# Two feed-forward units moved into the delta-rule recurrence, and the gate projection of the second batch moved between the parts of P @ u

## The reference

```python
xn = layernorm(x)
x + attention(xn) + feed_forward(xn)

# attention: 16 heads, key size 16, value size 32
q, k, v = silu(causal_conv4(xn @ W_qkv)); q, k = l2norm(q) * SCALE, l2norm(k)
beta = 2 * sigmoid(xn @ W_b + biases);  g = -exp(A_log) * softplus(xn @ W_a + dt_bias)
for t: S = S * exp(g_t); S += outer(k_t, (v_t - k_t @ S) * beta_t); o_t = q_t @ S
o = o * rsqrt(mean(o*o) + eps) * silu(xn @ W_g);  return o @ W_o

# feed forward: weights are 4-bit codes with one scale for 128 inputs; 1408 hidden features
h = silu(xn @ W_gate) * (xn @ W_up);  y = h @ W_down;  return y / sqrt(mean(y*y) + 1e-6)
```

## Time and profile before

| | |
|---|---|
| median of three runs | 3354.63 us |
| the profiled execution's own time | 3358.53 us |
| its span, first to last instruction | 3356.7 us |
| mean granted TensorE clock | 0.988 |
| busy: PE, DVE, ACT, POOL | 94%, 73%, 50%, 55% |
| chain that ended last, by engine | PE 64%, DVE 14%, issue 8%, POOL 6%, ACT 4% |

### The profile page before, as it was taken

One profiled execution on the slowest core, in us unless ns is written; L12 is line 12 of the kernel. 1 busy time (PEld: TensorE's weight loads), 2 busy tenths in 40 slices (PEclk: granted clock), 3 DMA queues, 4 the chain that ended last, 5 costly groups with the idle time before them and its releaser, 6 DMA issues.

```text
span 3356.7 us, 118358 instructions
## 1 busy us (share of the span) xinstructions
PE 3167.9 (94%) x45632; PEld 2247.1 (67%) x45632; DVE 2434.3 (73%) x5407; ACT 1666.1 (50%) x3306; POOL 1838.7 (55%) x2737
## 2 busy tenths in 40 slices
PE   4899999999999999999999999999999999999995
PEld 3666666766666766666666667666667666667663
DVE  7777777777777777777777777777777777777772
ACT  3444554545554445555445545455545455544452
POOL 3565455665455664456654456654556654456542
PEclk8999999999999999999999999999999999999996
DMA  3111111111111111111111111111111111111111
GB/s 111 39 46 27 34 44 35 45 38 28 40 40 39 46 33 30 43 33 45 46 27 37 43 33 45 45 28 34 43 36 46 37 28 42 37 42 46 33 25 30
DMA packets 318316, 132.07 MB, mean 39 GB/s; under 512 B 277088, under 2 KB 278880, under 8 KB 317792
## 3 DMA queue, kind: packets, MB, share of 16 engines
q1 hardware_dynamic: 313824, 119.26, 14.3%
q10 hardware_dynamic: 4096, 6.42, 0.5%
HBM read 75.30 MB, written 50.33 MB: 37 GB/s over the span
## 4 chain that ended last, share of the span: by engine, by line
PE 64%; DVE 14%; issue 8%; POOL 6%; ACT 4%; DMA 1%; ACTq 1%; DVEq 1%; SPq 0%; POOLq 0%
PE PS L1145 15%; PE PS L1210 7%; PE PS L1132 7%; PE PS L1133 6%; PE PS L1351 6%; PE PS L1100 5%; DVE arena L874 4%; PE PS L1275 3%; POOL arena L497 3%; POOL work L493 2%; DVE qkv L858 2%; DVE inner L976 2%; PE PS L1228 2%; PE PS L1196 2%; PE PS L1246 2%
## 5 line engine op out<-in xcount | busy, mean ns | idle before, releaser
L874 DVE SCALAR_TENSOR_TENSOR arena<-PS,sc,arena 128x256 f32<-128x256 f32 x2112 | 1004.5, 482 | 291.9 <-ACT arena L594 191.8
L1132 PE MATMUL PS<-xh,wgu 128*128 128x256 f32 x2816 | 872.0, 341 | 36.1 <-DVE arena L874 35.5
L594 ACT ACTIVATE arena<-PS,sc 128x256 f32<-128x256 f32 x704 | 330.8, 475 | 757.7 <-PE PS L1133 701.8
L1133 PE MATMUL PS<-xl,wgu 128*128 128x256 f32 x2816 | 699.3, 282 | 0.0
L1145 PE MATMUL PS<-wdn,inner 128*128 128x512 f32 x1408 | 650.7, 592 | 0.0
L1132 PEld LDWEIGHTS PS<-xh,wgu 128*128 128x128 f32 x2816 | 531.3, 189 | 156.2 <-issue 83.5
L1133 PEld LDWEIGHTS PS<-xl,wgu 128*128 128x128 f32 x2816 | 530.5, 188 | 83.2 <-issue 83.2
L497 POOL TENSOR_TENSOR arena<-arena,work 128x31 f32<-128x31 f32 (+15 forms) x992 | 543.3, 548 | 77.8
L493 POOL TENSOR_TENSOR work<-arena 128x31 f32<-128x31 f32 (+15 forms) x992 | 509.8, 514 | 138.9 <-DMA arena<-scr_a 63.7
L1100 PE MATMUL PS<-xnT,wqkv 128*128 128x256 f32 x2048 | 493.3, 389 | 25.6 <-ACT inner L574 24.8
L1100 PEld LDWEIGHTS PS<-xnT,wqkv 128*128 128x128 f32 x2048 | 379.5, 192 | 105.5 <-ACT inner L574 37.8
(11 more groups left out here) (141 smaller groups left out, 4546.8 us busy)
## 6 DMA issues: line engine op xcount, KB each, us to landing
xt<-in_x SPq DMA_DIRECT2D x64, 256.0 KB, 2.8
scr_a<-arena SPq DMA_DIRECT2D x64, 256.0 KB, 2.4
arena<-scr_a SPq DMA_DIRECT2D x256, 64.0 KB, 3.3
obuf<-in_x SPq DMA_DIRECT2D x64, 256.0 KB, 2.8
scr_t<-arena SPq DMA_DIRECT2D x32, 512.0 KB, 2.7
arena<-scr_t SPq DMA_DIRECT2D x256, 64.0 KB, 2.3
out<-obuf SPq DMA_DIRECT2D x64, 256.0 KB, 2.0
wqkv<-in_wqkv ACTq DMA_DIRECT2D x1, 2048.0 KB, 12.7
```

The source lines that it names most:

```text
L594: eng.activation(fa[:, u % 4, :], PS[:, bank(u, 0), 0:NB * P], ACT.Copy, scale=sc[:, u % 2, KB * m:KB * m + 1]).then_inc(fa_scaled.sem, 1)
L874: eng.scalar_tensor_tensor(out=fa[:, u % 4, :], in0=PS[:, bank(u, k // 2), k % 2 * NB * P:][:, 0:NB * P], scalar=sc[:, u % 2, KB * m + k:K ...
L1132: eng.matmul(o, w, xh[:, k, :], start=True, stop=False)
L1133: ins = eng.matmul(o, w, xl[:, k, :], start=False, stop=True)
```

## The change

`bank` is changed so that units 0 to 3 and 5 use banks 5 and 6 and units 4 and 6 banks 4 and 7. Both batches' gate sums and the transposes `turn_kb` and `turn_kqn(1)` use bank 4, one after the other, with the waits that this needs. Units 0 and 1 are put into the last two chunks of the recurrence on PE, and unit 2 before `p_times_u(1)`. `gate(1, ...)` stands between the parts of `p_times_u`. Units 4 and 5 stand ahead of `gram(1)`, unit 6 behind it. ACT's Silu table is loaded earlier, and its queue is put in a matching order. On DVE the statistics of the next layer norm go behind `conv(2)`, the normalisation behind `hidden(6)`, units 0 and 1 around `state(3)`, and units 3 and 4 with `hidden(0)` around the key products; the sums `so` come after `hidden(1)`. `turn_o`, `to_wo` and `result` come one or two units later, `down(1)` to `down(8)` one pair of units earlier. The orders of POOL and SP are as before.

```diff
         def bank(u, fill):
-            return (6 if u in (1, 3) else 2 if u % 2 else 4) + fill
+            if u < 7:
+                return ((4, 7) if u in (4, 6) else (5, 6))[fill]
+            return (2 if u % 2 else 4) + fill
...
 ACT
             decay(1)
+            eng.preload_act_table_set(SILU)
+            masked_keys(0)
             u_rows(2)
-            masked_keys(0)
+            gate_copy(0)
+            unit(0)
             u_rows(3)
             other_keys()
-            gate_copy(0)
-            gate_copy(1)
+            unit(1)
             masked_keys(1)
             queries()
-            unit(0)
-            unit(1)
+            unit(2)
+            if n:
+                gate(0)
             if t:  # copies of the output, after pu_out
...
-            unit(2)
+            unit(3)
+            gate_copy(1)
+            if n:  # Silu of v, moved up
...
             if t:  # Square of the output
...
-            unit(3)
-            eng.preload_act_table_set(SILU)
             if n:
-                gate(0)
-                ... Silu of v
                 unit(4)
-                gate(1)
                 unit(5)
-                ... Silu of the gate
-                gate(2)
+                gate(1)
+                unit(6)
...
+            gate(2)
+            ... Silu of the gate, behind the copies of v
...
 DVE
             conv(2)
+            if n and more:
+                layer_norm_stats(eng, n.next())
...
             state(2)
-            if n and more:
-                layer_norm_stats(eng, n.next())
+            unit(0)
             state(3)
-            if n and more:
-                layer_norm_apply(eng, n.next())
+            unit(1)
             conv(6)
...
-            unit(0)
-            unit(1)
             unit(2)
+            unit(3)
             gram_products(0)
+            hidden(0)
+            unit(4)
+            gram_products(1)
+            hidden(1)
             if t:  # the sums so
...
-            gram_products(1)
-            unit(3)
-            hidden(0)
-            hidden(1)
+            unit(5)
+            hidden(2)
...
 PE, half_unit
                     if fill == 0:
-                        eng.wait_ge(*gate_copied.at(n, NB))
+                        eng.wait_ge(*decay_done.at(n, NB))
...
+                    else:
+                        eng.wait_ge(*knq_copied.at(n, 2))
-                elif u == 1: ...
-                elif u == 5:
+                elif u <= 3:
+                    eng.wait_ge(*(fa_done if fill else fa_second).at(n, u))
+                elif u == 4:
+                    eng.wait_ge(*(q_copied.at(n, 1) if fill else gate_copied.at(n, NB)))
+                elif u == 7:
                     if fill == 0:
                         eng.wait_ge(*p_done.at(n, NB))
...
 PE, the order
             gate(0, 2)
+            gate(0, 3)
             k_times_u(2)
             q_times_s(2)
-            gate(0, 3)
-            gate(1, 0)
+            unit(0)
             y_times_s(3)
             turn_kb()
+            unit(1)
+            k_times_u(3)
+            q_times_s(3)
+            turn_kqn(1)
+            p_times_u(0)
+            turn_q()
+            unit(2)
+            p_times_u(1)
+            gate(1, 0)
             gate(1, 1)
-            k_times_u(3)
+            p_times_u(2)
             gate(1, 2)
-            q_times_s(3)
+            p_times_u(3)
             gate(1, 3)
-            p_times_u(0)
-            turn_kqn(1)
-            turn_q()
-            p_times_u(1)
-            unit(0)
-            p_times_u(2)
-            unit(1)
-            p_times_u(3)
-            unit(2)
+            unit(3)
             gram(0)
-            unit(3)
+            unit(4)
+            unit(5)
             gram(1)
-            unit(4)
...
+            unit(6)
             ... transposes of v
-            unit(5)
-            unit(6)
             unit(7)
             down(0)
+            unit(8)
+            down(1)
```

More of the change, by code:

```diff
@@ L636, in gate_copy @@
                 eng.wait_ge(*gate_out.at(n, b + 1))
-                eng.activation(gsn[:, b, :], PS[:, 4 + b, :], ACT.Copy).then_inc(gate_copied.sem, 1)
+                eng.activation(gsn[:, b, :], PS[:, 4, :], ACT.Copy).then_inc(gate_copied.sem, 1)
             def masked_keys(b):
@@ L752, in act_step @@
                     eng.activation(by_pair(sq[:, b, :]), paired(1, b), ACT.Copy).then_inc(o_copied.sem, 1)
-            unit(2)
+            unit(3)
+            gate_copy(1)
+            if n:
+                eng.wait_ge(*taps_done.at(n, NQKV))
+                eng.activation(qkv[:, 4:NQKV, :], qkv[:, 4:NQKV, :], ACT.Silu).then_inc(silu_done.sem, 1)
             if t:
@@ L778, in act_step @@
                                ACT.Copy).then_inc(v_copied.sem, 1)
+            gate(2)
+            if t:
+                eng.wait_ge(*o_gated.at(t, NB))
+            eng.wait_ge(*gate_copied.at(n, NB))
+            eng.activation(gs[:, :, :], gsn[:, :, :], ACT.Silu).then_inc(gs_done.sem, 1)
             for m in range(3, FM):
-                unit(2 * m)
+                if m > 3:
+                    unit(2 * m)
                 unit(2 * m + 1)
                 gate(m)
-                if m == 4:
+                if m == 5:
                     o_columns()
@@ L1039, in dve_step @@
                 return
-            for m in range(2, FM):
+            for m in range(3, FM):
                 unit(2 * m)
@@ L1045, in dve_step @@
                 hidden(m)
-                if t and m in (6, 8):
-                    result((m - 6) // 2)
+                if more and m == 6:
+                    layer_norm_apply(eng, n.next())
+                if t and m in (7, 9):
+                    result((m - 7) // 2)
             eng.wait_ge(*res_loaded.at(n, 16 * NB))
@@ L1288, in turn_kqn @@
                 for m in range(4):
-                    ins = eng.transpose(PS[:, 6, m * P:(m + 1) * P], kqn[:, b, m * P:(m + 1) * P], ident[:, :])
+                    ins = eng.transpose(PS[:, 4 if b else 6, m * P:(m + 1) * P], kqn[:, b, m * P:(m + 1) * P], ident[:, :])
                 ins.then_inc(kqn_turned.sem, 1)
@@ L1445, in pe_step @@
                 ins.then_inc(v_turned.sem, 1)
-            unit(5)
-            unit(6)
             unit(7)
             down(0)
-            for i in range(8, NU):
+            unit(8)
+            down(1)
+            for i in range(9, NU):
                 unit(i)
                 if i % 2:
-                    down((i - 7) // 2)
-                elif i == 8:
+                    down((i - 5) // 2)
+                elif i == 10:
                     turn_o()
-                elif i <= 16:
-                    to_wo((i - 10) // 4, (i - 10) // 2 % 2)
-            down(8)
+                elif 12 <= i <= 18:
+                    to_wo((i - 12) // 4, (i - 12) // 2 % 2)
             down(9)
```

25 lines of the change are left out of this document (8 added, 17 removed).

## The result

The kernel after takes 3584.9 us (median of four runs, 3575.4 to 3592.3) against 3353.65, a ratio of 1.0684 (95% interval 1.0669 to 1.0698). The profiled execution took 3589.75 us. Forecast were 3435 (3395 to 3480): the direction was right, and the loss is 231 us where 80 were foreseen. From one `yr` to the next a tile takes 109.17 us on the mean, before 101.68; 31 x 7.5 = 232, so it is all in the steady tiles.

A forecast was written before the change was run, and what follows sets the result against it. Two rings of about 101.5 us bound it, PE's work and solve-convolution-recurrence-key products. The second grows 2.8 less 0.25 spare: 31 x 2.55 = 79, first tile about 1; 3358.5 + 80, less 3.9, gives 3435 us (3395 to 3480).

The forecast's parts named there:

- The ring: Cycle of solve, convolution, recurrence, key products and next solve, about 101.5 us, forecast to grow by 2.8 us of a tile.
- The 9.55 from `so` to the solve: On POOL, `ro` with its long power, the scaling and two memsets were to take 9.55 us before the solve.
- the last term: Per-tile sum: the solve's 2.8 us delay less 0.25 us to spare, giving 2.55 us of a tile.
- the 2.8 forecast: On POOL, the solve was to begin 2.8 us later, because `so` ends later (1.9 to 3.4 by PE's holds).
- the 0.25 to spare: When PE's feed forward ends, the solve has been over for only about 0.25 us; that much delay was free.
- PE up to unit(3): PE's order from `turn_kqn(0)` on: 1607.4 without any stall, and with 0.9 of holds unit(3) begins at 1608.3.
- the wait for banks, 0.9: Units 0 to 3 share two banks, so PE waits for DVE to end the previous unit: 0.9 us (0 to 1.5).
- The wait for DVE: PE's waits for DVE at the units, 35.5 us in all before, were to shrink.
- Rival B: Clock falls each tile as PE stands before `project(3)`: 1.1 us of a tile, 3469 us; chance 0.15.
- A: PE's ring alone counts, saving 1.2 us of a tile: 3317 us; chance 0.10.
- C: Only the key products' read back delays the solve, 0.75 us of a tile: 3378 us; chance 0.10.
- D: No change, as PE's holds and savings cancel: 3355 us; chance 0.05.

## Why the prediction was wrong

**The sizes, separated.** In the kernel with 32 matmuls in each tile no tile has a stop, and the clock falls before S + 30 not at all, for 3.4 us, or for 6.8 us. The periods fall into groups. Added to the kernel after's own, they give each piece (the first and the last tile are left out, and three that are alone of their kind):

| tiles | count | mean period |
|---|---|---|
| before, all | 31 | 101.7 |
| 32 matmuls, no stop, no fall | 9 | 104.7 (104.7 to 104.8) |
| 32 matmuls, no stop, fall of 3.4 us | 9 | 105.65 (105.55 to 105.73) |
| 32 matmuls, no stop, fall of 6.8 us | 11 | 106.8 (106.3 to 106.9) |
| 64 matmuls, stops, one fall before S + 30 | 9 | 107.3 (106.8 to 107.8) |
| 64 matmuls, stops, one fall before S + 30 and one behind | 18 | 108.9 (108.3 to 109.5) |
| after, stops, one fall before S + 30 | 2 | 108.1 (107.7 and 108.4) |
| after, stops, one fall before S + 30 and one behind | 26 | 109.2 |

Ring 3.0, first fall 0.9, stops 2.5, second fall 1.1: 7.5 us of a tile. The stops and the fall that they bring, 3.6, are 112 us of 231, the largest part. How the 3.6 is to be split is not settled: 2.5 rests on two tiles and on kernels that differ by the pad, and by the kernel with 64 matmuls it would be 1.7 for the stops and 1.6 for the fall, 3.2 together. A fall of 3.4 us takes 1.7 us of clock. The first costs 0.9, probably because a part of that slow stretch waits for others anyway, the one behind the stops 1.1 to 1.6.

**The ring was right nearly step by step.** A tile of the kernel with 32 matmuls in each tile, without stop or fall, S = 1725.15 + 0.27 = 1725.42:

```profile
1725.15 0.27 POOL L499 TENSOR_TENSOR arena<-arena,work 128x31 f32<-128x31 f32 x1
1773.10 0.68 PE L1143 MATMUL PS<-xh,wgu 128*128 128x256 f32 x1
1781.19 1.27 DVE L1039 TENSOR_REDUCE so<-qkv 128x16 f32<-128x512 f32 x2
1792.17 0.24 POOL L495 TENSOR_TENSOR work<-arena 128x31 f32<-128x31 f32 x1 [0.34 <-POOL arena L487]
1830.22 0.19 POOL L509 TENSOR_SCALAR yr<-ys 128x2 f32<-128x2 f32 x1
```

unit(3) at S + 47.7 (forecast 48.0), `so` ending at S + 57.0 (56.8), the solve starting at S + 66.75 (66.4), a period of 104.7 (101.7 + 2.55 = 104.2). The 9.55 from `so` to the solve was 9.7. The missing 0.5 is in the last term: the start moves by the 2.8 forecast (from S + 64.0 on the mean), but the 0.25 to spare does not come off, and the solve takes 38.0 us instead of 37.7. Had nothing else happened, 31 x 3.0 + 1 would have made 3449 us, within the range.

**The step that failed is "PE up to unit(3)".** It ends at "1607.4 without any stall", and the only stall then allowed for was the wait for banks, 0.9. It laid `y_times_s(3)`, `turn_kb`, unit(1), `k_times_u(3)`, `q_times_s(3)`, `turn_kqn(1)` and `p_times_u(0)` behind each other at the durations they have with gate parts between them. Four gate parts had gone from there to the places between the `p_times_u`, and with them most of the time in which the next packet of instructions can arrive. The two stops (2.5) and the clock's fall behind them (1.1) stand in this step: unit(3) begins at S + 52.1 and, in the tile without stop or fall, at S + 47.7. No term of the sum and no rival had them. The wait for DVE, which I had put in it, did shrink: 24.2 us in 66 times against 35.5.

The warning was to be had. The kernel before has 12.4 us of stops at L1275 that no partner ends, 31 times, and I passed over them as too small. They were the largest row of PE's waits that named no partner, in 20 of 31 tiles, and nearly always after the same two rows, the 55th of `p_times_u(0)` and the 37th of `p_times_u(2)`; the row of 37 at 1604.39 ends at one.

The Trainium skill (Runtime: NRT & Kernel Launch, Instruction fetch mechanics) says that an engine's instructions are refilled in blocks of 16 KiB, 256 instructions, ahead and in order, and that crossing into the next block is "mostly hidden". The size agrees with the 16.4 KB and with the pads of 256 and 128; that it is mostly hidden does not hold where PE works off 256 instructions in 3.9 us (1705.11 to 1709.02 here): it stands 1.54 us at the end of them, and 0.89 at the end of those before.

**Rival B came as well.** It was priced at 1.1 us of a tile and not taken, because PE's stop was estimated at 3.4 us, "a little less than the 3.9 in the rows". The stop was 3.9 in the tile shown and in nearly all others, and the clock was low for a time before S + 30 in each of the 31 tiles. Its price was nearly right (0.9), its chance of 0.15 too low. The comparison of 3.4 with 3.9 us was no ground for leaving the clock up: in the kernel with 64 matmuls PE stood 2.7 us, and the clock fell in nearly every tile. Nor does the length of the gap alone decide: in the kernel with 32 matmuls, two tiles have the same gap of 3.3 us, and only in the second the clock falls. PE's timeline:

```profile
1731.08 1.99 PE L1109 MATMUL PS<-xnT,wqkv 128*128 128x256 f32 x8 [3.27 <-ACT inner L576]
1835.80 6.66 PE L1109 MATMUL PS<-xnT,wqkv 128*128 128x256 f32 x16 [3.26 <-ACT inner L576]
```

Their windows, the granted clock in the third column from the end:

```profile
1732.00:1734.00 2.00, 1.61 (x8) 1.08 (x7) 1.85 (x5) 1.96 (x5) 0.00 (x0) 1.00 0.73 115
1837.00:1839.00 2.00, 2.00 (x7) 1.55 (x6) 1.78 (x6) 1.75 (x4) 0.00 (x0) 0.50 0.80 125
```

The first goes on at a clock of 1.00, the second at 0.50. The same 16 matmuls take 4.4 us in the first (two rows of 1.99 with 0.39 between) and 6.66 in the second. The rule of the Trainium skill that is named beside rival B (TensorE: Matmul & The Clock Gate, HAM oscillation), that a loop which waits in every pass can start every pass throttled, is what the trace of after shows.

**Rivals A, C and D** are out by the start of the solve, S + 71.2. The range was too narrow because it held one cause at a time and the stops not at all. Ring, stops and clock come together: the ring's delay makes the gap before `project(3)`, and the stops bring the second fall. That the direction came out right is not luck, since the ring of the forecast is 3.0 of the 7.5 us.

**Left open.** Why a gap of 3.3 us sometimes lowers the clock and sometimes not, and why stops of the same length do so in half of the tiles of one kernel and in nearly all of another; how the 3.6 us divide between the stops and the fall behind them; why the solve takes 37.7 us before and 38.0 after.

## What to carry to other kernels

When small matmuls are gathered, ask what covers the arrival of their instructions: look in the waits for an engine that stops with no partner, always after the same row of the same operation, and keep large matmuls (a unit, a gate part) among each 256 instructions there. Before trusting a comparison of two orders, put a pad of 128 instructions ahead of the loop: if the time moves, a part of the difference is where the program lies. If it doesn't move, look where the stops went: they can cost as much elsewhere. And where two rings are of one length, a cheap reduction that one engine's chain needs should stand ahead of everything that this chain does not need.

## What the runs showed of the hardware

- TensorE's instructions come in packets of 16.4 KB, 256 instructions by the pads and by the distance of two stops, cut by place in the program; they come anew in each pass of the loop. A shift of 128 instructions ahead of the loop changed the time by 2.2% (3584.9 to 3504.9) with the loop unchanged.
- In rows of small matmuls (64 rows in 0.75 us) PE stood up to 2.2 us at a packet boundary. With the boundaries half a packet away, among gate parts and units, it did not stop in any of the 31 tiles.
- Two stops of about 0.9 and 1.7 us, no single one longer than 1.8, were followed by a fall of the clock in 28 of 30 tiles; without them no fall came there in any of 31. A single stop of 1.6 to 2.1 us was followed by one in 15 of 30 tiles.
- A fall of 3.4 us takes away 1.7 us of clock. It cost 0.9 us of a tile before S + 30, 1.1 to 1.6 behind the stops, and nothing at S + 58 to 60. After a gap of 2.7 us it came in 28 of 29 tiles, after gaps of 3.3 us in 20 of 29.
